# Routed experts computed only for the tokens that picked them, in 39 blocks of 256 rows

## What is computed

```python
xn = layernorm(x)                       # [4, 1024, 128]
# attention branch: 16 heads of 8 channels, elu+1, rotary turn, softmax, plus a 3-tap convolution of v
s = attention(xn) + lepe(v)
# expert branch
def mlp(x, g, W1, b1, W2, b2):          # W1: [experts, 128, 512], W2: [experts, 512, 128]
    h = gelu(rmsnorm(x, g) @ W1 + b1)
    return h @ W2 + b2
h_s = mlp(xn, g_shared, ...).sum(experts)          # 2 shared experts, every token
scores = sigmoid(xn @ centroids)                   # [tokens, 8]
gpk, i_topk = top_k(scores, 2)
gk = gpk / scores.sum(-1)
routed_all = mlp(xn, g_routed, ...)                # 8 routed experts, every token
h_r = (gk * routed_all[i_topk]).sum(experts)       # only 2 of the 8 are used
out = x + s * silu(xn + h_s + h_r)
```

## Time and profile before

| what | value |
|---|---|
| median of 3 runs | 1495.59 us (1494.63 to 1496.21) |
| the profiled execution's own time | 1497.12 us |
| its span | 1495.3 us, 1.8 us less than its own time |
| TensorE busy | 1422.5 us, 95% |
| VectorE, ScalarE, GpSimd busy | 843.1, 861.5, 351.3 us (56%, 58%, 23%) |
| mean granted clock | 0.971 |
| HBM read and written | 29.04 and 4.33 MB |

### The profile page before, as it was taken

How to read it: one execution, slowest core, us unless ns; L and a number is a source line. 1 busy time by engine, 2 the same in 40 slices (tenths; PEclk the granted TensorE clock), 3 DMA queues, 4 the chain that set the end, 5 groups by cost and what they waited for, 6 DMA issues and landing times.

```text
span 1495.3 us, 23800 instructions
## 1 busy us (share of the span) xinstructions
PE 1422.5 (95%) x6578; PEld 822.0 (55%) x6578; DVE 843.1 (56%) x1523; ACT 861.5 (58%) x1551; POOL 351.3 (23%) x435
## 2 busy tenths in 40 slices
PE   5699999999999994799999999999999999999998
PEld 4456566665666662455555555555555555555553
DVE  6421111112111113788887888888888888888881
ACT  5444444444444441067766766766766676676767
POOL 0022213122221215330330331232133033033000
PEclk9699999999999997599999999999999999999999
DMA  5111211112121110111011011101101101101100
GB/s 170 60 33 27 57 40 42 42 28 54 26 60 35 36 50 26 39 44 48 4 47 45 12 37 45 31 18 46 46 3 45 46 3 45 46 11 40 46 9 5
DMA packets 91416, 57.75 MB, mean 39 GB/s; under 512 B 38352, under 2 KB 85328, under 8 KB 90960
## 3 DMA queue, kind: packets, MB, share of 16 engines
q1 hardware_dynamic: 91344, 56.97, 15.2%
HBM read 29.04 MB, written 4.33 MB: 22 GB/s over the span
## 4 chain that ended last, share of the span: by engine, by line
PE 57%; DVE 2%; issue 1%; DMA 0%; ACT 0%; SPq 0%; ACTq 0%; POOLq 0%; POOL 0%; DVEq 0%
PE pa L1037 19%; PE pa L1049 17%; PE pa L1060 16%; PE pa L1083 2%; PE pa L1093 2%; PE pa L1088 1%; DVE neg_half L1184 1%; DVE feat L786 0%; ACT prob L1121 0%; PE pa L1077 0%; DVE w_cur L776 0%; DMA q_mask<-q_raw 0%; SPq L921 0%; DMA w_all<-in_wqkv 0%; SPq L932 0%
## 5 line engine op out<-in xcount | busy, mean ns | idle before, releaser
L1184 DVE TENSOR_REDUCE neg_half<-pa 128x1 f32<-128x512 f32 x1024 | 645.4, 684 | 128.7 <-PE pa L1060 115.6
L1121 ACT ACTIVATE prob<-pa 128x512 f32<-128x512 f32 x1024 | 545.1, 600 | 233.6 <-PE pa L1037 207.3
L1037 PE MATMUL pa<-q_sh,k_mask 128*128 128x512 f32 x1024 | 433.1, 428 | 5.3 <-ACT prob L1121 5.0
L1060 PE MATMUL pa<-k_raw,q_mask 128*128 128x512 f32 x1024 | 412.9, 409 | 0.5
L536 ACT ACTIVATE hidden<-ps,b 128x512 f32<-128x512 f32 x320 | 220.0, 688 | 278.4 <-PE ps L472 278.4
L1037 PEld LDWEIGHTS pa<-q_sh,k_mask 128*128 128x128 f32 x1024 | 191.4, 188 | 241.0 <-ACT prob L1121 189.0
L485 PE MATMUL ps<-hidden,w 128*128 128x512 f32 x640 | 322.9, 592 | 0.0
L1049 PE MATMUL pa<-prob,v_st 128*32 128x512 f32 x2048 | 272.7, 604 | 1.2 <-ACT prob L1121 0.7
L470 PE MATMUL ps<-xrh,w1h 128*128 (+1 forms) x320 | 245.8, 768 | 3.7 <-ACTq L521 3.7
L574 DVE SCALAR_TENSOR_TENSOR gated<-ps,b,gates 128x512 f32<-128x512 f32 x64 | 48.0, 751 | 315.8 <-PE ps L485 315.8
L1060 PEld LDWEIGHTS pa<-k_raw,q_mask 128*128 128x128 f32 x1024 | 196.4, 192 | 44.9 <-DVE neg_half L1184 17.6
(11 more groups left out here) (128 smaller groups left out, 776.7 us busy)
## 6 DMA issues: line engine op xcount, KB each, us to landing
gates<-gate_scratch SPq DMA_DIRECT2D x64, 256.0 KB, 4.5
k_mask<-k_raw SPq DMA_DIRECT2D x64, 128.0 KB, 2.5
q_sh<-q_raw SPq DMA_DIRECT2D x16, 512.0 KB, 3.1
q_mask<-q_raw SPq DMA_DIRECT2D x64, 96.0 KB
w<-in_w SPq DMA_DIRECT2D x1, 2560.0 KB, 9.8
w_in<-in_w SPq DMA_DIRECT2D x2, 1280.0 KB, 9.7
x_q<-in_x SPq DMA_DIRECT2D x4, 512.0 KB, 8.8
x_c<-in_x SPq DMA_DIRECT2D x8, 256.0 KB, 5.3
```

Source lines behind the costliest of these rows:

```text
L1037: nc.tensor.matmul(score_bank(n, par, s)[:, :], k_mask[par][:, j, kt * P:(kt + 1) * P], q_sh[par][:, qh * CH:(qh + 1) * CH], start=True, s ...
L1060: nc.tensor.matmul(m_ps[(k + par) % MB][:, :], q_mask[par][:, j, qt * P:(qt + 1) * P], k_raw[par][:, kh * CH:(kh + 1) * CH], start=True, s ...
L1121: nc.scalar.activation(prob[s // J % 2][:, j, :], score_bank(n, par, s)[:, :], ACT.Exp, scale=SCALE)\
L1184: nc.vector.tensor_reduce(out=neg_half[par][:, qt, j, kh:kh + 1], in_=m_ps[(k + par) % MB][:, :], axis=AX.X, op=ALU.max, negate=True)\
```

## The change

The routed experts leave the 8 chunks. The prologue also computes, for each token and each of its two experts, a row number (`keep["slot"]`), so that all tokens of an expert stand together in blocks of 256 rows. Every expert's rows begin at a new block, so that 4096 x 2 / 256 + 7 = 39 blocks always suffice, and all 39 are always run. Rows of a block with no token are zero: the prologue writes zeros over the scratch tensor `slots` (5.1 MB, three transfers). It also computes which expert each block has (`keep["expert"]`).

In the experts block 8 units of 512 tokens run the 2 shared experts (8 hidden tiles each). Beside them GpSimd scatters the normed tokens into `slots` with 64 indirect transfers (32 tiles of 128 tokens, two experts each). After them 39 units follow, one per block, with 4 hidden tiles of 256 columns. For each, SyncE reads the expert's number into a register and loads w1, the rows, w2, b1 and b2; the rows are transposed (`prepare`), weights and rows are split into high and low parts (`split`), and the answers are stored to `answers`. Two buffers of each kind (`SPARE`). The down product now has the hidden tile of 128 tokens as its stationary operand and w2 (128 columns) as its moving one, so its answers come out as tokens x channels. LAG is 2 in place of 3. The loops are written out.

In the attention block GpSimd gathers a batch's two answers per token with 16 indirect transfers (`gather`, for batch b in item 4b - 1), VectorE multiplies each by its gate and adds it (`add_picked`, 16 operations in slots 8 to 23 of item 4b), ScalarE takes the tanh in slot 28, and GpSimd makes silu and adds x (`silu`, four operations of 128 x 1024). The copies `x_cur` and `w_cur`, the tile `q_sh` and `rest_scratch` go. The rounds for q and k move from slots 47 to 61 of item n to slots 3 to 11 of item n+1. All items are written out, no loop. The diff, cut to its core:

```diff
+TOPK = 2
+RB = 256
+RT = RB // P
+ROUTED = TOPK * NTOK // RB + ER - 1
...
+            nc.vector.tensor_tensor(both[:, :, :], pick[0][:, :, :], pick[1][:, :, :], ALU.add).then_inc(both_ok, 1)
...
+            step(nc.vector.tensor_copy(of_tile[:, :, :], tiles_ps[:, 0:TILES * ER].rearrange(by_expert, e=ER)))
...
+            step(nc.vector.tensor_tensor_scan(running[:, :, :].rearrange("p e t -> p (e t)"),
+                                              of_tile[:, :, :].rearrange("p e t -> p (e t)"),
+                                              zero[:, 0:TILES * ER], 0.0, ALU.add, ALU.add))
+            step(nc.vector.tensor_copy(upto[:, :], running[:, :, TILES - 1]))
...
+            step(nc.vector.reduce_sum(which[:, :], past[:, :, :], axis=AX.X))
+            step(nc.vector.tensor_scalar(keep["expert"][:, :], which[:, :], float(ER - 1), None, ALU.min))
...
+            step(nc.vector.tensor_tensor(slot[:, :, :],
+                                         within_ps[:, 0:TILES * ER].rearrange("p (t e) -> p t e", e=ER),
+                                         running[:, :, :].rearrange("p e t -> p t e"), ALU.add))
+            for k in range(TOPK):
+                step(nc.vector.tensor_tensor(part[:, :, :], slot[:, :, :], pick[k][:, :, :], ALU.mult))
+                step(nc.vector.reduce_sum(slot_f[k][:, :], part[:, :, :], axis=AX.X))
+                step(nc.vector.tensor_copy(keep["slot"][:, k, :], slot_f[k][:, :]))
...
+            e_now = [sp.value_load(keep["expert"][0:1, k:k + 1], min_val=0, max_val=ER - 1) for k in range(2)]
+            def load(k):
+                i, e = k % SPARE, e_now[k % 2]
+                if k >= SPARE:
+                    sp.wait_ge(x_lo_ok, k - SPARE + 1)
+                    sp.wait_ge(w_lo_ok, k - SPARE + 1)
+                sp.dma_start(w_raw[i][:, :], io["w1"][:, bass.ds(e + ES, 1), :].rearrange("p a n -> p (a n)"))\
+                  .then_inc(w1_in[i], 16)
+                sp.dma_start(x_tok[i][:, :, :], x_v[k, :, :, :]).then_inc(x_in[i], 16)
+                if k >= SPARE:
+                    sp.wait_ge(down_ok, hids_before(SHARED + k - SPARE + 1))
+                    sp.wait_ge(y_out, SHARED + k - SPARE + 1)
+                sp.dma_start(w_2[i][:, :], io["w2"][:, bass.ds(e + ES, 1), :].rearrange("p a n -> p (a n)"))\
+                  .then_inc(w2_in[i], 16)
+                sp.dma_start(b_1[i][:, :], io["b1"][:, bass.ds(e + ES, 1), :].rearrange("p a n -> p (a n)"))\
+                  .then_inc(w2_in[i], 16)
+                sp.dma_start(b_2[i][:, :], io["b2"][bass.ds(e + ES, 1), :].broadcast_to([P, C]))\
+                  .then_inc(w2_in[i], 16)
+            def store(k):
+                sp.wait_ge(y_out, SHARED + k + 1)
+                sp.dma_start(y_v[k, :, :, :], y_tok[k % SPARE][:, :, :]).then_inc(y_st[k % SPARE], 16)
+            sp.wait_ge(moved_in, 16 * TOPK * TILES)
+            for k in range(ROUTED):
+                load(k)
+                if k >= SPARE:
+                    store(k - SPARE)
+                if k + 2 < ROUTED:
+                    e_now[k % 2] = sp.value_load(keep["expert"][0:1, k + 2:k + 3], min_val=0, max_val=ER - 1)
+            for k in range(ROUTED - SPARE, ROUTED):
+                store(k)
+            for i in range(SPARE):
+                sp.wait_ge(y_st[i], 16 * ((ROUTED + SPARE - 1 - i) // SPARE))
...
+        def _(pool):
+            for t in range(TILES):
+                for k in range(TOPK):
+                    nc.gpsimd.indirect_dma_start(out=io["slots"], out_offset=bass.IndirectOffsetOnAxis(
+                        ap=keep["slot"][:, k, t:t + 1], axis=0), in_=ffn["xr_all"][:, t, :], in_offset=None)\
+                      .then_inc(moved_in, 16)
+            pool.wait_ge(moved_in, 16 * TOPK * TILES)
...
+            def prepare(k):
...
+                if k >= 2:
+                    pe.wait_ge(x_lo_ok, k - 1)
+                for t in range(RT):
+                    last = nc.tensor.transpose(aux[k % 2][:, t * P:(t + 1) * P], x_tok[k % SPARE][:, t, :],
+                                               ident[:, :])
+                last.then_inc(aux_full, 1)
...
+            def down(u, q):
+                n = hids_before(u) + q
+                bank = y_ps[u % 2]
+                if q == 0:
+                    if u >= 2:
+                        pe.wait_ge(y_out, u - 1)
+                    if u >= SHARED:
+                        k = u - SHARED
...
+                    w2 = w_2[(u - SHARED) % SPARE][:, q * P:(q + 1) * P]
+                pe.wait_ge(gelu_ok, n + 1)
...
+                last.then_inc(down_ok, 1)
...
+            order = steps()
+            for i in range(len(order) + LAG):
+                if i < len(order):
...
+                        turn(u // 2)
+                    if next_at(u, q):
+                        prepare(u + 1 - SHARED)
+                if i >= LAG:
+                    down(*order[i - LAG])
         @block.scalar
         def _(act):
...
+            def split(k):
+                i = k % SPARE
+                act.wait_ge(w1_in[i], 16 * (k // SPARE + 1))
+                if k >= SPARE:
+                    act.wait_ge(hid_full, hids_before(SHARED + k - SPARE + 1))
+                nc.scalar.activation(w_hi[i][:, :], w_raw[i][:, :], ACT.Copy).then_inc(w_hi_ok, 1)
+                act.wait_ge(aux_full, k + 1)
+                nc.scalar.activation(x_hi[i][:, :], aux[k % 2][:, 0:RB], ACT.Copy,
+                                     scale=ffn["gain_r"][:, 0:1]).then_inc(x_hi_ok, 1)
...
+            def output(u):
+                dve.wait_ge(down_ok, hids_before(u + 1))
...
+                else:
+                    k = u - SHARED
...
+                    dve.wait_ge(w2_in[k % SPARE], 48 * (k // SPARE + 1))
+                    nc.vector.tensor_tensor(y_tok[k % SPARE][:, :, :], y, over_tiles(b_2[k % SPARE][:, :], u),
+                                            ALU.add).then_inc(y_out, 1)
+            def split(k):
+                i = k % SPARE
+                dve.wait_ge(w_hi_ok, k + 1)
+                nc.vector.tensor_tensor(w_lo[i][:, :], w_raw[i][:, :], w_hi[i][:, :].bitcast(F32),
+                                        ALU.subtract).then_inc(w_lo_ok, 1)
+                dve.wait_ge(x_hi_ok, k + 1)
+                nc.vector.scalar_tensor_tensor(x_lo[i][:, :], aux[k % 2][:, 0:RB], ffn["gain_r"][:, 0:1],
+                                               x_hi[i][:, :].bitcast(F32),
+                                               ALU.mult, ALU.subtract).then_inc(x_lo_ok, 1)
...
+                if q == LAG and u > 0:
+                    output(u - 1)
+                if next_at(u, q):
+                    split(u + 1 - SHARED)
...
+            def gather(b):
+                if b > 0:
+                    pool.wait_ge(added, KT * TOPK * b)
+                for k in range(TOPK):
+                    for t in range(KT):
+                        nc.gpsimd.indirect_dma_start(out=picked[k][:, t, :], out_offset=None, in_=io["answers"],
+                                                     in_offset=bass.IndirectOffsetOnAxis(
+                                                         ap=keep["slot"][:, k, b * KT + t:b * KT + t + 1], axis=0))\
+                          .then_inc(picked_in, 16)
...
+            def add_picked(b, i):
+                k, t = i // KT, i % KT
+                if i == 0:
+                    dve.wait_ge(picked_in, 16 * KT * TOPK * (b + 1))
+                if i == KT:
+                    dve.wait_ge(added, KT * TOPK * b + KT)
+                tile = b * KT + t
+                nc.vector.scalar_tensor_tensor(acc[:, tile, :], picked[k][:, t, :], keep["gate"][:, k, tile:tile + 1],
+                                               acc[:, tile, :], ALU.mult, ALU.add).then_inc(added, 1)...
-    AT_SHIFT1, AT_QKV, AT_K, AT_Q, AT_SHIFT0, AT_LAST_OUT = 23, (13, 17), (47, 51), (57, 61), 54, 7
+    AT_SHIFT1, AT_QKV, AT_K, AT_Q, AT_SHIFT0, AT_LAST_OUT = 23, (13, 17), (3, 5), (9, 11), 54, 7
+    GATHER_AT, ADD_AT, TANH_AT = 0, 8, 28
```

More of the change, by code:

```diff
@@ L179, in _ @@
+            blank = io["slots"].rearrange("(g p r) c -> g p (r c)", p=P, r=rows)
+            for g in range(ROUTED * RB // (P * rows)):
+                sp.dma_start(blank[g, :, :], zero[:, :]).then_inc(zero_st, 16)
+            sp.wait_ge(zero_st, 16 * (ROUTED * RB // (P * rows)))
+            sp.wait_ge(ffn_in, 96)
+        @block.gpsimd
+        def _(pool):
+            nc.gpsimd.memset(zero[:, :], 0.0).then_inc(zero_ok, 1)
         @block.vector
         def _(dve):
-            dve.sem_inc(xrT_out, 2)
@@ L475, in down @@
-            def down(c, par, q):
-                e, ht = q // HT, q % HT
-                y = max(0, e - ES + 1)
-                first, last = q in (0, *range(ES * HT, NQ, HT)), ht == HT - 1 and e >= ES - 1
-                bank = y_ps[(par + y) % 2]
-                m = slice(ht * P, (ht + 1) * P)
-                if first:
-                    pe.wait_ge(y_out, c * NY + y + 1)
```

(12 more changed lines are left out.)

767 lines of the change are left out of this document (379 added, 388 removed).

## The result

The changed kernel took **1434.4 us** (median of 4 runs, 1432.05 to 1436.51) against 1495.8 before: ratio 0.959, 95% interval 0.957 to 0.961, so 61 us faster. The forecast was 1457.

The account below looks back on a forecast made before the run. TensorE was taken to bound experts and attention, with VectorE a close second in attention. Span 537.4 to the attention plus 919.3 gave 1456.7; with 1.8 outside, less 1.5 for the median, 1457 us; range 1400 to 1535.

Parts of the forecast that it names:

- Prologue and shared units: Before the routed units: prologue 57.4 becomes 62.4 us, then 64 shared tiles with extras take 117 us, ending at 179.4.
- Scatter: GpSimd's 64 indirect transfers beside the shared units: 1.3 us each, some 83 us, hidden up to 1.83 each.
- the scatter is late: Rival, chance 0.10: at 2.3 us per transfer the scatter ends 30 us behind the shared units; 1503 us in all.
- Routed units: 39 blocks after the shared units: 36 turns at 9.3 us plus 20 for the ends, 355 us, bounds 305 to 435.
- The ring: Routed stage: answer k-2 releases SyncE's loads, rows of k+1 land, then answer k-1 follows; 9.3 us per block.
- the register load: SyncE's read of the expert number within each routed block's turn: 1.0 us taken, from 0.2 to 2.0.
- The loop is dearer: Rival, chance 0.22: SyncE's issues and register load at their upper bounds, 11.2 us per routed block, 1525 us in all.
- Loads run ahead: Rival, chance 0.10: TensorE paces the routed stage at 3.7 us per block, 144 us; 1246 us in all.
- Attention: Attention stage: 912.5 becomes 919.3 us, +6.8 from loops, start, additions and first gather.
- The additions: VectorE's 16 add_picked operations in the attention: 3 us per batch, +12 us in all, bounds 0 and 22.
- The loops' turns: Attention items written out: 1.0 us saved in each of 6 or 7 turns, -6.5 us.
- The start: Attention's start: copies go but feat stays held until GpSimd's last memset; -1.2 us, bounds -3.5 and 0, before additions.

Follow-up runs that it names:

- g1: f3 with the tokens of block k+1 transposed and split after the third up step of block k, not the fourth: 1287.0 us, 4.50 us a block.
- e2: Changed kernel with the expert number of block k+2 read into a third register ahead of the wait for answer k-2: 1436.0 us.
- e1: Changed kernel with w_raw and x_tok of block k+1 issued before the wait for answer k-2: 1404.1 us, 7.27 us a block.
- a1: Changed kernel with the attention's shifts for item n+1 placed ahead of the store of result n's first half on SyncE: 1420.5 us.
- e3: Changed kernel with tokens of block k+1 transposed after the last up step of block k, not its second: 1344.5 us, 5.69 us a block.
- f3: Changed kernel with the edits of e1, e3 and a1, and the b2 rows of all eight routed experts kept in SBUF: 1316.1 us.
- g2: f3 with the tokens transposed and split after the second up step, as in the changed kernel: 1344.7 us, 6.03 us a block.
- h1: Changed kernel without the routed b2 load from block 2 on, plus e2's earlier register read: 1395.5 us, 7.05 us a block.

## Why the prediction was right, and where it was off

The mechanism and the sign were right; the sum was 27 us too high (span 1430.0 against 1456.7), in three pieces. That it came so near is partly luck: the routed stage was forecast 42 us too long and the attention 17 us too short. With the attention as forecast the measured time would have been some 1417 us, below the stated range.

- **Prologue and shared units**, 179.4 forecast, 177.3 measured. The routing chain took what it should (45.87 to 62.60), the first `up` came at 63.48 instead of 62.4, and the 64 tiles with their extras 114 us instead of 117. The zeros cost nothing, as priced; they had landed by 27.6 us, not near 50.
- **Scatter**: forecast 1.3 us each, measured 1.27 (0.96 and 0.30 of "issue"). The last was issued at 144.93, well ahead of the last shared unit, so *the scatter is late* is out. The Trainium skill ("DMA: Bandwidth & Descriptors", "Anatomy of one DMA") gives about 2.0 us fixed for one such transfer. The trace agrees, with 2.2 us from issue to landing, but the 128 us that the prediction worked out for transfers one behind the other did not come: the next is issued before the one ahead of it has landed.
- **Routed units**, the term that was mis-sized: 9.3 us for each of 36 turns forecast, 8.25 measured, 38 us, and 4 less at the two ends, 42 us in the stage. The ring is as it was written down. Its pieces, forecast and as means of the 36 turns: from the answer's end to x_tok's issue 4.1, measured 3.35; landing 2.7, measured 3.0 up to the transposes; from there to the end of the next answer 2.5, measured 1.9. In the first piece the register load was most of the error (0.56, not 1.0); the issues stand 0.38 to 0.53 apart, not 0.6. In the last it was the clock: the forecast took 1.2 GHz throughout and expected 0.5 to 0.6 for the stage, but 0.83 was granted, in turns at 1.2 and at 2.4 GHz, with TensorE busy 59% of the time. On the register load, the floor of about 600 ns that the Trainium skill ("DMA: Bandwidth & Descriptors", "Latency and other measured facts") states for a `tensor_load` was the better number; the 0.56 measured here lies just below it. *The loop is dearer* falls with 3.35 us to x_tok's issue. *Loads run ahead* was the better kernel, not this one: g1 comes to 4.5 us a block where that rival said 3.7, though TensorE's own work, 3.6 us there, was forecast well at 3.5.
- One price was wrong in kind. The prediction took landing as a constant of 2.7 us and each SyncE step as worth its own length. e2 shows that it isn't: 0.56 us off the queue came back as 0.6 us of landing. And it saw one ring where the orders hold two; ScalarE's, through the biases, lay 0.75 us a block below the first, so that e1, which opens the first alone, gave 30 of the possible 134 us (g1 against a1). e3 opens both with one line and gave 90.
- **Attention**, 919.3 forecast, 936.6 measured, against 912.5 before: +24.1 instead of +6.8. The additions came as priced (2.85 and 3). What the forecast put at nothing were the late shifts, 12.6 us. They follow from what stands above on the kernel before, that a transfer waits in SyncE's queue behind every wait written ahead of it; I costed the gathers on GpSimd as covered, without asking who waits for GpSimd's `combine` behind them. The loops' turns gave back only 4.1 us where 6.5 was expected (five turns, three of 0.96 to 1.01 and two of 0.55 to 0.60), and written-out items 1, 5 and 9 took 53.97 instead of 53.7. The start took 90.4 us up to its first pv_sb, 2.0 more than before, where +4.3 was forecast with batch 0's additions. Behind the last store's issue 5.4 us pass to the end of the span where 2.3 did before. The trace names what these 3.1 us wait for: GpSimd's `DRAIN` at the end of the block (line 753) starts at 1423.93 and takes 5.80 us, where the kernel before has 0.56 (line 665). Why it is longer stays open.

## What to carry to other kernels

When stages of two buffers run on several engines, write down each engine's program order and look for *every* circle that closes over one block; a buffer count says nothing about it, and opening one circle shows only the next. Then place the next block's preparation just behind the last work of the block before: here one step later cost 29 us (f3 against g1), one step earlier 58 (g2 against g1). And when long work goes on an engine with slack, ask what stands behind it in that engine's queue, and what stands in the next queue behind the one that waits for that.

## What was not expected of the hardware

- A transfer that reads one row of 512 bytes for all 128 partitions (64 KB) held up those issued around it: 64 GB/s on the core in the 2 us behind w2's burst at 357. Leaving it out was worth 0.80 us a block, of which 0.3 in the landing of others.
- Issuing transfers earlier need not bring them earlier: 0.56 us earlier came to 0 with that transfer (e2) and about half of it without (h1).
- An indirect transfer costs GpSimd 0.96 us and 0.30 behind it (64 of 128 x 512 bytes), writes and reads of rows alike (0.94 and 0.30 for the gather); it lands 2.2 us after its issue, while the next ones go out.
- GpSimd's `DRAIN` takes 5.30 and 5.80 us at the end of the two blocks in which it issues indirect transfers, in the changed kernel and all its variants alike; before the change it took 1.38 and 0.56. In the attention that is 3.1 us at the end of the program. Whether it is the indirect transfers was not told apart.
- In the stretch 200 to 350 the granted clock was 0.82 in the changed kernel and 1.00 in g1, with TensorE busy there 88 and 120 of 150 us.
